# A two-layer decoder's first phase: bank-fed convolution, products and softplus on VectorE, state output by channel, absolute exponents on ScalarE

## What is computed

```python
x = x + L0_attn(layernorm(x))          # Mamba-like, 32 heads of 16 channels, state of 128
#   proj = x @ in_proj_w.T -> x_ssm (512), z (512), B (128), C (128), dt (32)
#   x_ssm = silu(depthwise conv of 4 taps over time + conv_b)
#   dt = softplus(dt_in + dt_bias);  A_bar = exp(-exp(A_log) * dt)
#   h = A_bar * h + dt * B * x_ssm;  y = C . h + Dp * x_ssm
#   out = (rmsnorm(y) * norm_w * silu(z)) @ out_proj_w.T
x = x + L0_xattn(layernorm(x), ctx, mask)   # 16 heads of 16
router and shared part of L0_ffn(layernorm(x))   # softmax of 16 logits, top 2, shared silu(x@Sg)*(x@Su)@Sd
```

## Time and profile before

| | |
|---|---|
| median of 3 executions | 4792.0 us (4787.19 to 4794.8) |
| span of the profiled execution | 4774.6 us |
| phase 1, two and three (rough) | 0 to 2480, 2480 to 2720, 2720 to 4775 us |
| busy over the span: PE, DVE, ACT, POOL | 88%, 70%, 60%, 57% |
| mean granted TensorE clock | 0.949 |
| one round of phase 1, most often | 37.5 us |
| one round at full clock throughout | 35.9 us |

### The profile page before, as it was taken

The page is one execution under the profiler, slowest core; times in us unless marked ns, Lnnn a source line. Parts: engine busy times, 40 slices in busy tenths (PEclk is TensorE's granted clock), DMA queues, the critical chain, the costliest instruction groups (busy, mean ns, idle before and its releaser), DMA issues.

```text
span 4774.6 us, 119919 instructions
## 1 busy us (share of the span) xinstructions
PE 4215.5 (88%) x34006; PEld 3007.4 (63%) x34071; DVE 3359.3 (70%) x8668; ACT 2885.5 (60%) x7026; POOL 2721.2 (57%) x4093
## 2 busy tenths in 40 slices
PE   5888888888888888888869979999999999999998
PEld 3666555665565565665547756666666666666665
DVE  4667666777767766667635557777777787777776
ACT  3666666666666666666634446666666666666564
POOL 5666666666666666666622335555555555555554
PEclk8989999999999999999979989999999999999999
DMA  3222232222222222222224401111111111111110
GB/s 112 89 88 89 95 103 78 75 75 98 76 75 75 85 88 76 75 75 84 89 67 144 133 24 32 31 31 31 31 31 30 29 30 31 29 30 31 31 31 18
DMA packets 222142, 304.10 MB, mean 64 GB/s; under 512 B 56720, under 2 KB 175760, under 8 KB 222096
## 3 DMA queue, kind: packets, MB, share of 16 engines
q1 hardware_dynamic: 197632, 249.83, 16.7%
q0 software_dynamic: 19200, 52.45, 3.4%
q10 hardware_dynamic: 5264, 1.25, 0.1%
HBM read 239.19 MB, written 64.23 MB: 64 GB/s over the span
## 4 chain that ended last, share of the span: by engine, by line
PE 58%; DVE 19%; issue 11%; POOL 6%; ACT 4%; DMA 1%; DVEq 1%; ACTq 1%; POOLq 1%; SPq 0%
PE Q L1427 21%; PE Q L1432 10%; PE Q L1420 5%; PE Q L1470 4%; DVE arena L832 4%; DVE arena L830 3%; PE Q L1777 3%; PE Q L1810 3%; PE Q L1629 3%; PE Q L1461 3%; PE Q L1455 2%; DVE arena L860 2%; DVE mx L782 2%; PE Q L1641 2%; POOL arena L640 1%
## 5 line engine op out<-in xcount | busy, mean ns | idle before, releaser
L1432 PE MATMUL Q<-ident,arena 128*128 128x128 f32 x4768 | 803.8, 292 | 155.3 <-ACT arena L1176 69.4
L1432 PEld LDWEIGHTS Q<-ident,arena 128*128 128x128 f32 x4768 | 557.2, 146 | 390.1 <-issue 146.0
L1427 PE MATMUL Q<-Wkvl,arena 128*128 128x512 f32 x1024 | 500.3, 601 | 0.0
L640 POOL TENSOR_TENSOR arena<-arena 128x1024 f32<-128x1024 f32 x256 | 479.5, 1890 | 14.3 <-DMA arena<-cum_rows 14.3
L704 POOL TENSOR_TENSOR l<-l,half_pow 128x8 f32<-128x8 f32 x192 | 318.5, 1659 | 233.0 <-DVE l L1057 231.2
L729 POOL TENSOR_TENSOR arena<-arena,part_of 128x512 f32<-128x512 f32 x256 | 263.8, 1041 | 190.8 <-DVE part_of L1095 190.6
L782 DVE TENSOR_REDUCE mx<-Q 128x4 f32<-128x512 f32 x512 | 344.0, 682 | 11.3 <-PE Q L1455 6.6
L1470 PE MATMUL Q<-arena 128*17 128x128 f32 x4096 | 244.5, 312 | 115.5 <-ACT arena L1193 115.5
L1461 PE MATMUL Q<-ident,arena 128*128 128x128 f32 x2048 | 301.4, 280 | 13.2 <-ACT arena L1193 11.4
L1461 PEld LDWEIGHTS Q<-ident,arena 128*128 128x128 f32 x2048 | 231.4, 142 | 122.9 <-issue 75.7
L1186 ACT ACTIVATE arena<-Q,mx 128x128 f32<-128x128 f32 x1024 | 281.8, 373 | 1.0 <-DVE mx L782 1.0
(11 more groups left out here) (311 smaller groups left out, 10677.9 us busy)
## 6 DMA issues: line engine op xcount, KB each, us to landing
arena<-cum_rows SPq DMA_DIRECT2D x256, 512.0 KB, 6.6
arena<-routed_rows SPq DMA_DIRECT2D x144, 128.0 KB, 2.1
expert_rows<-arena POOLq DMA_DIRECT2D x144, 128.0 KB, 2.0
arena<-in_x_dram SPq DMA_DIRECT2D x128, 128.0 KB, 5.0
arena<-in_ctx_dram SPq DMA_DIRECT2D x128, 128.0 KB, 6.6
x_rows<-arena SPq DMA_DIRECT2D x128, 128.0 KB, 1.7
arena<-x_rows SPq DMA_DIRECT2D x128, 128.0 KB, 2.4
out_dram<-arena SPq DMA_DIRECT2D x64, 128.0 KB, 1.7
```

The costliest lines, as they stand in the source:

```text
L640: tell(g.tensor_tensor(E8[j], E8[j], cums[:, 8 * j:8 * j + 8].unsqueeze(2).broadcast_to([P, 8, T]), ALU.subtract), "diff")
L1427: last = mm(out, lhs(c), rhs(c), start=c == 0, stop=c == n - 1)
L1432: last = nc.tensor.transpose(out[:, c * P:(c + 1) * P], src[:, c * P:(c + 1) * P], ident[:, :])
```

## The change

In words, all of it in phase 1:
1. `xpad` goes. ACT reads the projection's bank and makes the last tap with the bias (`conv0`, four instructions with scale and bias); DVE adds the other three taps, reading the bank (12 instructions).
2. The series runs on DVE: `Msp` and `Msp6` to `Msp0`, 11 further steps, each linked to the last. POOL's 13 go.
3. The masked `CB` stays in a bank (bank 4), and all four products with it are DVE's (L833), none POOL's. `bc` moves to bank 4 and now waits for the fourth product.
4. `xdt` has 32 columns for each head, 16 of them zero, and pairs of heads add up in one bank, by channel: no copies, no turning back, one bank less. `y2`, `gz`, `z` are by channel too; Dp is a scalar for each channel. The sum of squares is made by PE (`Nss`).
5. Cross-attention: all four groups take the maximum on DVE and exp with bias on ACT (before, two of them were subtracted by DVE first). The head output is scaled in its bank. Chain W (the norm and query part of X) stands apart.
6. Router: both top values come from one maximum of the raw logits, ahead of the exp. The shared part is computed turned, so that `hT` falls away.
7. The norm's POOL part has three steps instead of four. The ten `awake` matmuls go. All five order tables are written anew.

The core of the diff:

```diff
 ORDER[1]["DVE"]
-    Fln3 Xln2 Nm0 Mln1 Fr Yk Ftop Mdt Fslot Msp Xm0 Xm1 Fhg Nm1 Nm2 Xm2 Xm3 Fxo Vcv Vcv1 Vcv2 Vcv3 Ny0 Vxs2 Ny1 Vcb Vxdt Vgz Nx1 Xho
+    Fln3 Wln2 Nm0 Yk Mln1 Fr Ftop Nm1 Fslot Nm2 Xm0 Nm3 Mdt Xm1 Msp Msp6 Msp4 Msp2 Msp0 Fhg Xm2 Xm3 Vcv1 Fxo Ny Vcv2 Vcv3 Vxs2 Nss Vcb Vxdt Xho Vgz Nx1
 ORDER[1]["ACT"]
+    Ne0 YcT Nf0 Ne1 Fln3 Xmr Yv Fln3n Wln2 Nf1 Wln2n Frx Ne2 Wq Nf2 Ne3 Mln1 Nf3 Mln1n Xm0 Mab Fth Vbc Xm1 Vcv Mcum Xm2 Xm3 Xt0 Xt1 Nsq Xt2 Xt3 Vcth XOT Vtz
@@ DVE
-                tell(v.tensor_tensor(dts[:, 2, :], u, dts[:, 5, :], ALU.mult), "ratio")
+                s, z, tail_of = dts[:, 2, :], dts[:, 3, :], dts[:, 4, :]
+                J(v.tensor_tensor(s, u, dts[:, 5, :], ALU.mult))
+                J(v.tensor_tensor(z, s, s, ALU.mult))
+                J(v.tensor_scalar(tail_of, z, 2.0 / (2 * TERMS - 1), None, ALU.mult))
+                for k in range(TERMS - 2, 0, -1):
+                    if k % 2 == 0:
+                        yield f"sp{k}"
+                    J(v.scalar_tensor_tensor(tail_of, tail_of, 2.0 / (2 * k + 1), z, ALU.add, ALU.mult))
+                yield "sp0"
+                J(v.scalar_tensor_tensor(tail_of, tail_of, 2.0, s, ALU.add, ALU.mult))
+                J(v.scalar_tensor_tensor(dts[:, 6, :], dts[:, 0, :], 0.0, tail_of, ALU.max, ALU.add))
+                tell(v.tensor_tensor(dts[:, 7, :], dts[:, 6, :], Aneg[:, :], ALU.mult), "a")
...
+                    for c in range(IC):
+                        late = xc[:, c * T + shift:(c + 1) * T]
+                        k = NCONV - 1 - shift
+                        last = v.scalar_tensor_tensor(late, Q[1][:, c * T:(c + 1) * T - shift], convw[:, c, k:k + 1], late, ALU.mult, ALU.add)
...
-                v.tensor_tensor(heads(xdt), heads(Q[1][:, :]), wide(dts[:, 6, :]), ALU.mult)
-                tell(v.tensor_tensor(heads(xD), heads(Q[1][:, :]), wide(Dpb[:, :]), ALU.mult), "xdt")
+                tell(v.tensor_tensor(pairs(xdt), Q[1][:, :].rearrange("p (i k w) -> p i k w", k=2, w=HP),
+                                     dts[:, 6, :].rearrange("p (i k) -> p i k", k=2).unsqueeze(3).broadcast_to([P, NH // 2, 2, HP]), ALU.mult), "xdt")
...
-                for j in range(3):
+                for j in range(4):
                     yield f"m{j}"
                     done(dve, "E", b, j + 1)
+                    done(dve, "cbm", b)
+                    tell(v.tensor_tensor(E8[j], E8[j], Q[4][:, 3 * T:4 * T].unsqueeze(1).broadcast_to([P, 8, T]), ALU.mult), "M")
+                yield "y"
+                done(dve, "Yk", b, 4)
+                for c in range(IC):
+                    o = slice(c * T, (c + 1) * T)
+                    last = v.scalar_tensor_tensor(y2[:, o], th0[:, o], Dch[:, c:c + 1], Q[3][:, o], ALU.mult, ALU.add)
@@ ACT
-                tell(s_.activation(xpad[:, :, NCONV - 1:], cut(Q[1][:, :], IC), ACT.Copy), "xpad")
+                for c in range(IC):
+                    last = s_.activation(xc[:, c * T:(c + 1) * T], Q[1][:, c * T:(c + 1) * T], ACT.Identity, bias=convb[:, c:c + 1], scale=convw[:, c, NCONV - 1:])
@@ PE
-                awake(Q[0][:, 0:2 * T], 5)
...
                 yield "bc"
                 done(pe, "ln1_T", b)
-                was(pe, "gz", b)
+                was(pe, "M", b, 4)
...
-                        awake(Q[3][:, :], 5)
...
+                    for k in range(2):
+                        for i in range(k, 8, 2):
+                            h = 8 * j + i
+                            r = 16 * (i - k)
+                            last = mm(Q[3][r:r + 32, j * T:(j + 1) * T], xdt[:, h * 32:h * 32 + 32], E8[j][:, i, :], start=k == 0, stop=k == 1)
```

325 lines of the change are left out of this document (139 added, 186 removed).

## The result

The changed kernel took 4471.8 us in the median of four executions (4444.98 to 4476.66), the kernel before 4791.6; the ratio is 0.9324, with a 95% interval of 0.9298 to 0.9349. I had forecast 4605 and a range of 4470 to 4720. So the direction was right, but the gain, 6.8%, was well over my 3.9%, and the time lies at the lower end of the range.

The account below looks back on a forecast made before the run. No engine is full; a path through several queues sets the round. Full-clock stretches sum to 33.0 us, 34.25 with the clock, against 37.17; 183 us off span 4774.6 gives 4592, plus 17.4 is 4609, stated as 4605, range 4470 to 4720.

Parts of the forecast that it names:

- A: End of `x1` to start of the convolution: 20.28 us before, forecast 20.0 at full clock.
- B: The convolution, with `xo` and `y2` among its taps after the change: 6.84 us before, forecast 5.1.
- C: End of the convolution to end of `x1`: 8.80 us before, forecast 7.9.
- The clock: TensorE's clock below full was taken to cost 1.25 us a round, as much as before the change.
- rival 1: Clock low longer, scores to dt: +2 us in half the rounds, +4 in all; 4655 to 4780 us; chance 0.22.
- Filling and draining: Five rounds filling and draining the loop gain half a round's gain each, 8 us; loading costs 3 us.
- The 17.4 us: Distance of the runs' median above the profiled span, added to the forecast span 4592 to give 4609.
- Rival 2: DVE's 14 linked softplus steps become the bound at 0.58 us each: 38.65 us a round, 4885 us; chance 0.08.
- Rival 4: Change misses the path; loads or POOL's subtractions set the round: 37.2 us a round, 4790 us; chance 0.03.
- Rival 3: ACT's stretch closes up and the clock does not fall: 31.5 to 32.5 us a round, 4430 to 4500; chance 0.15.
- The rule on the ports: DVE instructions with two SBUF inputs contend with POOL reading SBUF; taps, products and `y2` reading a bank would be free.
- What would show it: Signs: reciprocals 34.2 apart, norms 2 us after `x1`, 14 steps in 3.7, taps at most 0.3, `z` 4 after taps.

Follow-up runs that it names:

- a_awake_early: Also "the base": changed kernel plus six unread matmuls, three behind `x1`, three before PE's wait for the query projection; 4343.2 us, ratio 0.9065.
- after_again: The changed kernel run once more with no edit; 4444.2 us, ratio 0.9279 to the kernel before.
- b_m3_dve: Kernel before the change, with the product of piece 3 moved from POOL to DVE, ahead of the taps; 4704.3 us, ratio 0.9813.
- e_m3_pool2: a_awake_early with piece 3's product back on POOL, masked `CB` in SBUF, `bc` waiting only for that `CB`; 4457.7 us, ratio 0.9323.
- e_xpad_conv: a_awake_early with the convolution fed as before: ACT copies into padded SBUF, DVE does all four taps; 4571.7 us, ratio 0.9544.

## Why the prediction was right and wrong

- **The three stretches** were the right marks. At full clock (a_awake_early) they measure A 18.77, B 4.78, C 7.02, 30.57 together, where I had 20.0, 5.1, 7.9, 33.0. This sum is the step that failed, in its sizes: 2.43 us a round, 148 us over 61.
- **A, short by 1.23.** The fourth product starts at 11.69 (I had 12.0, from ACT's queue): 0.31. The 14 steps took 3.20 and not 3.75: a linked step is 0.22 to 0.23, not 0.27, which I had read from one pair of the router's steps: 0.55. Maxima, dt and gate: 0.22. The last 0.15 I had added by rounding 19.85 up.
- **B, 0.32.** The 12 taps cover 3.41 us (I had 3.5), `xo` and `y2` 1.37 (1.5), and 0.1 was rounding. A tap from the bank costs what I said, that of one from SBUF: both start 0.26 apart within a group of four; my 0.29 was a mean with the links between the groups.
- **C, 0.88.** `z` starts 3.32 us after the last tap, not 4.0, which is 0.68: half of the output projection (1.03 us) ends with `Vxdt`, and the head transposes begin before its end, where I had stacked them. From `z` to the end of `x1` it is 3.70, not 3.9.
- **The clock.** I kept its price at 1.25 us a round, as before. That term failed too. The stretch it belonged to, ahead of `z`, is at full clock now, and a new one took its place, from the queries to the shared part: 32.65 - 30.57 = 2.08 us in the profiled run and 1.4 in the second. That is rival 1's place and sign. It had 2 us for half of the rounds and 4 for all; the clock was low in 60 of 61, at about half that price. It stands 51 us on the other side of the account, so the two errors partly cancel: 2.43 - 0.83 = 1.6 us a round, the 34.25 forecast against 32.65.
- **Filling and draining** I put at 8 us less 3. Outside of the 61 rounds 24.8 us were gained, 20 more than that. Of the 9.1 us behind the last `x1` 5.6 are there when the experts' first gather starts (49.4 us after it instead of 55.0); where the rest comes from, no run here shows.
- **The 17.4 us** that I added to the span were the distance of one quick profiled execution from the median of others. The changed kernel's median lies 3.2 us below its profiled span: 21 us of the miss of 133 are this term, some 97 the rounds, 20 filling and draining, less the 4 that I had rounded off.
- **Rival 2**, a linked step at 0.58, fell: 0.22. Rival 4 fell. Rival 3, to which I gave 0.15, is where the time lies (4430 to 4500; after_again's 31.99 is in its 31.5 to 32.5 a round, the first profile's 32.65 just outside). Of its two conditions one held in part, ACT's stretch closed up by 0.3 us, and the other did not: the clock fell, and the work was shorter by more than that. So its number came out by other means than it named.
- **The rule on the ports** stood in the prediction with no term of its own, though 2.1 of the 3.31 us that I took for the first taps were one tap's wait for POOL. That wait is worth 1 us a round net of the product that DVE takes over (b_m3_dve), and undoing it in the base costs 1.8 us (e_m3_pool2).
- **What would show it:** reciprocals 32.7 apart, not 34.2; norm at 2.2 us (I had 2.0); steps in 3.2 us; taps 0.26 apart; `z` at 3.3; POOL's idle time in the phase 1076 us instead of 818, a third more, as I had it. Of the signs of being wrong that I named the first came: a granted clock of 0.89 in the phase, with the scores' rows at nearly double length.

## What to carry to other kernels

Before costing a deleted matmul "with no use" at nothing, look where PE is thin after the change and what stands behind that stretch: here six unread ones in the right place gave 101 us, ten in the old places 46, and six in the kernel before, where the low stretch was covered, none. Take the step time of a linked chain from a chain of the same engine and size, several steps long. And before moving an operation on one engine, look at the queue that issues its DMA: an addition moved by 3.4 us cost 4 us a round (a part of it by the clock), because the loads of the next round stood behind its store.

## What the runs showed of the hardware

- An operation of DVE or POOL that is held by the other's waits to the other's end, whatever its own size: 0.35 became 1.48 us, 0.27 became 0.99 (e_m3_pool2), a tap of 0.34 became 1.35 (e_xpad_conv).
- The masked `CB` in a bank instead of in SBUF frees both engines at no cost to the product itself: 1.22 us and 1.23.
- A stop of PE of 3.3 us was followed by matmuls at half speed (2.08 us for 1.13), and which rounds are hit can differ between executions of one kernel by enough to move its time 0.6%.
